# A selective scan block: four of sixteen drive units made on GpSimd as u times B, the opening in halves, the last residual added in HBM

## The reference

```python
x = x + ln(attn(ln(x), ...));  x = x + ln(ffn(ln(x), weight, bias))       # ln: eps 1e-5

def attn(x, ...):                        # d_inner 256, d_state 16, 4 taps
    x_in, z = split(x @ W_in + b_in)
    xc = silu(causal_conv4(x_in) + conv_b)
    Bm, Cm = split(xc @ W_xp + b_xp)     # 16 columns each
    delta = softplus(xc @ W_dt + b_dt)
    dA  = exp(delta[..., None] * -exp(A_log))
    dBx = (delta * xc)[..., None] * Bm[:, :, None, :]
    h_t = dA_t * h_(t-1) + dBx_t;  y_t = sum_s h_t * C_t      # over 256 tokens
    y = (y + D_skip * xc) * silu(z)
    r = x + y @ W_out + b_out
    return alpha * (r - mean(r)) / (std_unbiased(r) + 1e-6) + beta

def ffn(x, weight, bias):                # fake_quant: per-tensor fp8 e4m3 and back
    return fake_quant(x) @ fake_quant(weight).T + bias
```

## Time and profile before

| | |
|---|---|
| median of 3 runs | 639.04 us |
| the profiled execution | 639.14 us |
| its span | 637.4 us |
| PE busy | 542.6 us, 85% |
| DVE busy | 504.8 us, 79% |
| ACT busy | 441.9 us, 69% |
| POOL busy | 300.7 us, 47% |
| transfers of the POOL queue (additions into `acc`) | 33.56 MB, 26.7% of 16 engines |
| transfers of the SP queue | 5.78 MB, 3.3% |

### The profile page before, as it was taken

The page is one execution under the profiler, slowest core; times in us unless marked ns, Lnnn a source line. Parts: engine busy times, 40 slices in busy tenths (PEclk is TensorE's granted clock), DMA queues, the critical chain, the costliest instruction groups (busy, mean ns, idle before and its releaser), DMA issues. The chain is left out here.

```text
span 637.4 us, 10358 instructions
## 1 busy us (share of the span) xinstructions
PE 542.6 (85%) x2893; PEld 419.1 (66%) x2893; DVE 504.8 (79%) x1001; ACT 441.9 (69%) x885; POOL 300.7 (47%) x333
## 2 busy tenths in 40 slices
...
DMA packets 19184, 39.84 MB, mean 62 GB/s; under 512 B 3648, under 2 KB 9920, under 8 KB 19136
## 3 DMA queue, kind: packets, MB, share of 16 engines
q0 software_dynamic: 9216, 33.56, 26.7%
q1 hardware_dynamic: 9920, 5.78, 3.3%
...
## 5 line engine op out<-in xcount | busy, mean ns | idle before, releaser
L1200 DVE TENSOR_TENSOR_SCAN state<-decay,drive 128x512 f32<-128x512 f32 x256 | 297.2, 1203 | 30.7 <-PE drive L995 24.9
L995 PE MATMUL drive<-diag,uT 128*128 128x256 f32 x1024 | 245.9, 384 | 0.7 <-ACT uT L731 0.7
L745 ACT ACTIVATE decay<-delta,a_neg 128x510 f32<-128x510 f32 x256 | 170.5, 730 | 54.8 <-DVE state L1200 53.9
L995 PEld LDWEIGHTS drive<-diag,uT 128*128 128x128 f32 x1024 | 187.1, 193 | 21.7 <-ACT uT L731 1.0
L1011 PE MATMUL hT<-ident,state 128*128 128x128 f32 x1024 | 143.0, 278 | 24.3 <-DVE acc_d L1223 19.1
L1011 PEld LDWEIGHTS hT<-ident,state 128*128 128x128 f32 x1024 | 119.8, 143 | 56.3 <-issue 26.1
L500 POOL TENSOR_SCALAR_AFFINE_SELECT diag<-Bt 128x512 f32<-128x512 f32 x128 | 92.1, 725 | 74.5 <-PE drive L995 58.2
L766 ACT ACTIVATE term<-hT,Ct 128x256 f32<-128x256 f32 x256 | 102.9, 484 | 8.8 <-PE hT L1011 8.8
L516 POOL DMA_DIRECT2D acc<-term x64 | 59.9, 935 | 24.1 <-DMA acc<-term 11.8
L1223 DVE SCALAR_TENSOR_TENSOR acc_d<-hT,Ct,acc_d 128x256 f32<-128x256 f32 x160 | 66.5, 470 | 4.4 <-PE hT L1011 4.3
L938 PE MATMUL fbank<-xnT,w_tap 128*128 128x512 f32 x112 | 50.4, 592 | 0.0
...
## 6 DMA issues: line engine op xcount, KB each, us to landing
acc<-term POOLq DMA_DIRECT2D x64, 512.0 KB, 4.5
out_dram<-state SPq DMA_DIRECT2D x8, 256.0 KB, 2.2
x_all<-in_L_attn_x_dram SPq DMA_DIRECT2D x2, 256.0 KB, 4.2
state<-in_L_attn_conv_w_dram SPq DMA_DIRECT2D x1, 512.0 KB, 5.4
w_in<-in_L_attn_W_in_dram SPq DMA_DIRECT2D x1, 256.0 KB, 3.2
w_dt<-in_L_attn_W_dt_dram SPq DMA_DIRECT2D x1, 256.0 KB, 5.1
...
```

The source lines that it names most:

```text
L745: last = nc.scalar.activation(decay[:, g % DECAYS, h, :, s, 1:], delta[:, par, h, :, 1:], ACT.Exp, scale=a_neg[:, h, SG * g + s:SG * g + s ...
L995: last = nc.tensor.matmul(dst[:, :, P * c:P * c + P], uT[:, par, TC * b + c, P * h:P * h + P], diag[:, n % DIAGS, c, :, :], start=True, st ...
L1200: nc.vector.tensor_tensor_scan(state[:, n % STATES, h, :, :].rearrange("p s t -> p (s t)"), decay[:, g % DECAYS, h, b, :, :].rearrange("p ...
```

## The change

Groups MADE = (2, 5), that is units 4, 5, 10 and 11 of each pair, no longer get a diagonal or a matmul. SP writes the B columns of such a group to HBM in rows (`b_rows`, 1,024 pieces of 4 bytes), loads them back spread over all partitions (`b_all`, 512 KB) and POOL multiplies: `made` = u * B, one operation of 128 x 512 a half. DVE scans these units from `made` in SBUF instead of `drive` in PSUM. `b_all` has one buffer, `made` one for each sequence. The other twelve units keep their way, with LEAD 2 instead of 3 and DIAGS 3 instead of 4. To make room, `pre` shares the memory of `dt_v`, and `ysumT` is gone: the sums stay in `acc`. Twenty-three places in the dictionaries move.

In the opening, `w_tap` is built ahead of the fp8 scaling, the load of `cw_r` goes from seventh to fourth place, Silu reads the bank directly, and the softplus chain, `delta`, `u` (now on DVE) and `uT` run in halves.

In the tail POOL no longer adds the residual: SP stores x1 (the sum behind the first block) to the output during the slots, and POOL issues an additive transfer of each normalized group to HBM, from four buffers.

The diff, cut to its core:

```diff
-LEAD = 3
+LEAD = 2
-DECAYS, DIAGS, STATES, TERMS = 2, 4, 4, 4
+DECAYS, DIAGS, STATES, TERMS = 2, 3, 4, 4
+MADE = (2, 5)
+DRIVEN_G = tuple(g for g in range(DS // SG) if g not in MADE)
-POOL_STEPS = dict(front_root=(3,), front_residual=(24,), front_u=(25,), back_gate=(11,), back_affine=(21,),
-                  back_sum=(25,), sum_states=(6,), back_root=(13, 22, 27))
+POOL_STEPS = dict(front_root=(5,), front_residual=(26,), front_u=(25,), back_gate=(8,), back_affine=(19,),
+                  back_sum=(25,), sum_states=(5,), back_root=(15, 21, 26))
...
             sp.dma_start(w_in[:, :], W_in).then_inc(w_in_loaded, 16)
-            sp.dma_start(bin_c[:, :], column(b_in), **slow).then_inc(w_in_loaded, 16)
+            sp.dma_start(cw_r[:, :, :], conv_w.rearrange("(o d) a k -> o d (a k)", o=1).to_broadcast([P, DI, TAPS])).then_inc(tap_loaded, 16)
...
+            def spread_b(pr, par):
+                sp.wait_ge(bc_ready, nth(pr, 3, 2))
...
+                    sp.dma_start(b_rows[k].rearrange("r p -> p r"),
+                                 Bt[:, par, g, :, :, :].rearrange("p b c s -> p (b c s)"), **slow).then_inc(b_stored[k], 16)
+                for k, g in enumerate(MADE):
+                    sp.wait_ge(b_stored[k], nth(pr, 16, 16))
+                    if k:
+                        sp.wait_ge(made_ready, nth(pr, MADES, PAIR * HALVES * k))
...
+                    sp.dma_start(b_all[:, :, :, :, :].rearrange("p b c s t -> p (b c s t)"),
+                                 b_rows[k].rearrange("(o r) p -> o (r p)", o=1).to_broadcast([P, SG * TOK]))\
+                        .then_inc(b_spread[k], 16)
+            def store_x1(pr):
+                sp.wait_ge(b_sum, nth(pr, 1, 1))
+                sp.dma_start(out_v[:, bass.ds(pr.v * CH, CH), :], x_k[:, bass.ds(pr.v * CH, CH), :]).then_inc(x1_stored, 16)
...
+            def make_drive(pr, par, n):
+                pool.wait_ge(u_ready, nth(pr, 1, 1))
+                pool.wait_ge(b_spread[k], nth(pr, 16, 16))
...
+                for h in range(HALVES):
+                    u_h = u[:, h, L * b:L * b + L].rearrange("p (c t) -> p c t", c=TC).unsqueeze(1).to_broadcast([P, SG, TC, P])
+                    nc.gpsimd.tensor_tensor(made[:, b, h, :, :].rearrange("p s (c t) -> p s c t", c=TC), u_h,
+                                            b_all[:, b, :, :, :].rearrange("p c s t -> p s c t"), ALU.mult).then_inc(made_ready, 1)
             def diag_b(pr, par, n):
+                if g in MADE:
+                    make_drive(pr, par, n)
+                    return
...
-            def last_sum(grp, par):
+            def add_to_out(grp, par):
                 pool.wait_ge(f_norm, nth(grp, 1, 1))
-                nc.gpsimd.tensor_tensor(fo[:, par, :], fn[:, par, :], x_all[:, bass.ds(grp.v * TOK, TOK)], ALU.add)\
-                    .then_inc(f_out, 1)
+                pool.dma_start(out_v[:, CH * grp.v:CH * grp.v + CH, :], chunks(fn[:, grp.v % 4, :]), accum_op=ALU.add)\
+                    .then_inc(stored[grp.v % 4], 16)
...
             for h in range(HALVES):
-                front_xin(Pair(0), h)
+                act.wait_ge(front_full, 1 + h)
+                nc.scalar.activation(xc[:, 0, h, :], front_bank(Pair(0), h), ACT.Silu, bias=in_bias[:, h:h + 1])\
+                    .then_inc(xin_ready, 1)
...
             def drive_unit(pr, par, n):
+                if g in MADE:
+                    return
...
+                if g in MADE:
+                    dve.wait_ge(made_ready, nth(pr, MADES, HALVES * turn(MADE, n) + h + 1))
+                    new = made[:, b, h, :, :].rearrange("p s t -> p (s t)")
+                else:
+                    new = drive[:, m % 2, h, :]
                 nc.vector.tensor_tensor_scan(state[:, n % STATES, h, :, :].rearrange("p s t -> p (s t)"),
                                              decay[:, g % DECAYS, h, b, :, :].rearrange("p s t -> p (s t)"),
-                                             drive[:, n % 2, h, :], 0.0, ALU.mult, ALU.add).then_inc(scan_done, 1)
+                                             new, 0.0, ALU.mult, ALU.add).then_inc(scan_done, 1)
...
+            for h in range(HALVES):
+                dve.wait_ge((half_log, sp_log)[h], 1)
+                nc.vector.tensor_tensor(d[:, h, :], dt_v[:, h, :], dt_e[:, h, :], ALU.max)\
+                    .then_inc((half_delta, delta_ready)[h], 1)
+                dve.wait_ge((half_delta, delta_ready)[h], 1)
+                nc.vector.tensor_tensor(u[:, h, :], d[:, h, :], xc[:, 0, h, :], ALU.mult).then_inc((half_u, u_ready)[h], 1)
```

More of the change, by code:

```diff
@@ L132, in turn, with unit @@
     return PAIR * groups.index(n // PAIR) + n % PAIR
+def unit(groups, j):
+    return PAIR * groups[j // PAIR] + j % PAIR
 def directs(j, s, c):
@@ new lines, in store_x1 @@
+            def store_x1(pr):
+                sp.wait_ge(b_sum, nth(pr, 1, 1))
+                sp.sem_inc(sp_waited, 1)
+                sp.dma_start(out_v[:, bass.ds(pr.v * CH, CH), :], x_k[:, bass.ds(pr.v * CH, CH), :]).then_inc(x1_stored, 16)
+            spread_b(Pair(0), 0)
+            with sp.Fori(0, (PAIRS - 2) // 2) as i:
+                for k in range(2):
+                    pr = Pair(i * 2 + (1 + k), 1 + k)
+                    spread_b(pr, 1 - k)
+                    store_x1(pr.plus(-1))
@@ L454, in _ @@
+            spread_b(Pair(PAIRS - 1), 1)
+            store_x1(Pair(PAIRS - 2))
+            store_x1(Pair(PAIRS - 1))
+            sp.wait_ge(x1_stored, 16 * PAIRS)
+            for k in range(4):
+                sp.wait_ge(stored[k], 16 * PAIRS // 4)
         @block.gpsimd
```

214 lines of the change are left out of this document (131 added, 83 removed).

## The result

The changed kernel takes **670.1 us** (median; 669.6 to 672.1) against 638.0 for the kernel before beside it: ratio **1.049 [1.045, 1.053]**. The forecast was 614.5 with a range to 634: wrong in direction. Its profiled execution has a span of 667.9 us.

The account below looks back on a forecast made before the run. PE was taken to bound slots 0 to 6, DVE slot 7. Opening -8.8, slot 0 -4.6, slots 1 to 6 -7.8, slot 7 +3.5, last back part 0, tail -6.9: -24.6 from 639.1 gives 614.5 us, range 595 to 634.

Parts of the forecast that it names:

- no holding: Rival: scans from SBUF are not held, or wait where DVE idles anyway; 590 us, chance 0.18.
- A slot is 57.4 + 4.2 = 61.6: Slots 1 to 6, before holding: DVE becomes the bound, its 57.4 us of work plus slot 7's idle 4.2.
- PE falls to 54.5: Steady slots: four of sixteen drive units leave PE, 1.91 us each, so PE loses 7.65 us a slot.
- only the edges gain: Rival: middle slots stay at 66.4 us because waits between engines make up the slot; 622 us, chance 0.20.
- The nearest row is 0.44 a time ... I take 3.5: Each slot: eight made scans held by POOL on SBUF cost 3.5 us, bounded by 0 and 10.2.
- POOL takes the bound's place: Rival: each made scan meets a whole POOL read, and POOL's reads wait in turn; 661 us, slower, chance 0.10.
- 3.0 to 6.0, and I take 4.5: Slot 0: time in us for B's store in 4-byte pieces, taken from bin_c's 512 pieces in 3.0.
- Slot 0: First slot: PE relieved, but DVE stalls 3.1 us because B comes late; 57.8 instead of 62.4, -4.6 us.
- Slot 7: Last slot: already bound by DVE, gains nothing and pays for held scans, +3.5 us (0 to +10).
- The opening: Before the first scan: earlier loads and shorter chains, first scan at 34.8 instead of 43.6, -8.8 us.
- The tail: Final groups: POOL's residual addition no longer slows DVE's mask and fshift, -6.9 us; the last addition to HBM counted 0.
- a mean 0.4 above 1.2 us: Sign in slots 1 to 6: made scans average this much while the other scans do not.

Follow-up runs that it names:

- f2: Changed kernel without B's store and load (b_all constant), POOL's products kept, but the scans of the four made units read a drive bank in PSUM: 618.3 us, ratio 0.968.
- e2: Changed kernel with b_all filled once with a constant, so no store, load or wait for B; products and SBUF scans kept: 653.8 us, ratio 1.025.
- f3: Changed kernel without B's store and load and without POOL's products, the four made units' scans reading PSUM: 618.1 us, ratio 0.966.
- e1: Changed kernel with B stored in 128 pieces of 32 bytes a group instead of 1,024 of 4 bytes: 650.9 us, ratio 1.019.
- h1: Changed kernel whole, with its transfers and products, but the four made units' scans read a drive bank in PSUM: 623.7 us, ratio 0.977.
- e3: Changed kernel with no made units: PE drives all sixteen, four diagonal buffers, new places, opening and tail kept: 624.2 us, ratio 0.978.
- f1: Changed kernel without B's store and load and without POOL's products; made is a constant that the four units' scans read in SBUF: 638.9 us, ratio 1.001.

## Why the prediction was wrong, by its steps

A ledger from the forecast to the result, from differences of runs. Without holding and without transfers the forecast was 590 and f2 measured 618.3: 28.3, of which 4.1 a slot, taken six times, are about 25 and the end of the tail some 4. Holding was forecast at 24.5 and is 35.5 (e2 - f2): 11.0. Transfers were forecast at nothing beyond slot 0 and are 16.3 (670.1 - e2). 614.5 + 28.3 + 11.0 + 16.3 = 670.1; it closes because it is a chain of differences. The terms stand for this order of taking things away: with the scans in PSUM the transfers are 5.4 and the holding 46.4.

1. **"A slot is 57.4 + 4.2 = 61.6": failed, about 25 us.** I took slot 7's idle time of DVE as what remains in a middle slot once PE is relieved. f3 and f2 have exactly that state, and a slot is 65.7: in f3 DVE is busy 57.0 us of it, as forecast, and idle 8.7, not 4.2. These four us a slot are waits between the engines; that slot 7 lacks them because no next pair is prepared there is argued, not shown. PE's own relief was smaller as well: "PE falls to 54.5" became 59.1 in f3 and 61.2 in the changed kernel, with granted clocks of 0.95 and 0.93. The rival *only the edges gain* (66.4 a slot, 622) was right on this term. The forecast for f3's state would have been the 590 of the rival *no holding*; it measured 618.
2. **"The nearest row is 0.44 a time ... I take 3.5": the size of a meeting was right, what it does was not; 11 us without transfers.** 64 `made` scans took 64 x (1.601 - 1.203) = 25.5 us extra, 0.40 each (forecast 0.44), and 7 x 3.5 = 24.5 was the forecast for seven slots. But the term priced DVE's side only, and the runs put holding at 35.5 (e2 - f2). POOL's reads are held in turn, twice as much in sum (50 us), and its in-order queue hands that to diagonals, gate and roots; it comes back to DVE as 12.9 us more of waiting. I had that mechanism as the rival *POOL takes the bound's place*, with 661 as its time, and gave it 0.10 because "0.44 is what a meeting costs". `shift` is a 0.16 us instruction: it can be held by POOL, but hardly holds POOL. A scan of 1.2 us does. The row couldn't show the second half.
3. **"3.0 to 6.0, and I take 4.5" for the store, "some 26 us for 10: hidden", and "nothing" for its load on the transfer engines: failed, 16 us.** The two stores took 9.2 us in slot 0 and 11.6 to 12.4 in the later ones, and the addition behind them 12.7 where it had been 5.2 to 5.9; POOL waits for that landing with all its queue. The row I went by, `bin_c`, was one transfer of 512 pieces; here 2,048 pieces go, and in the later slots 512 KB additions with them. The load on the transfer engines was priced in bytes, and should have been in pieces.
4. **Slot 0: half failed.** 61.9 and not 57.8: with the store at 9.2, POOL waited 3.6 us for `b_all` and DVE 5.0 for the root (forecast 3.1), and PE was busy 55.4, not 52.8. **Slot 7: right**, 57.2 against 58.5.
5. **The opening: right.** 35.6 against 34.8; `w_tap` at 8.3 (7.8).
6. **The tail: the gain right, its end wrong.** -6.0 of -6.9, and +4.5 where I wrote 0: I took the landing of an addition as *at most* 4.5 and set it against the whole of addition, store and 2.2; it was 5.1, and 9.0 from the last normalisation to the end.

The forecast's test "a mean 0.4 above 1.2 us" for `made` scans came true in a kernel that lost 5%: a sign that an operation costs what was expected is no sign that the sum holds. The Trainium skill (SBUF — State Buffer, "Who interferes with whom") was read rightly as "all eight scans, and POOL's products too, queue for one port", and the runs agree with that sentence (2.18 and 3.42 us above). My sum left out the second half of it, POOL's products.

A repair that keeps the plan would have to let POOL write its products into the drive banks in PSUM, where f2 scans them for nothing. The Trainium skill (PSUM — Partial Sum Buffer, "The four PSUM rules") says that GpSimd can't touch PSUM at all; no run here shows it, and it wasn't tried.

**Left open.** Why the addition beside the 4-byte stores lands after 12.7 us. It goes with the pieces (the same addition takes 5.8 to 6.4 in e2, 7.8 to 9.1 in e1) and not with held scans: POOL's waits for it are still 48.3 us in h1, where no scan has two SBUF inputs. No run moved the stores to another place of the slot. Twice, where the hardware loop starts its next round, ACT stands too, for 7.84 and 8.6 us, and the profile names nothing for it; these are the two slots of 77 us, the others are 68 to 70. Only a part of that can be this wait: in e3 the same slots are longer too, 68.5 against 64.5.

## What to carry to other kernels

Before work goes from a full engine to one with room, ask where the *consumer* will read the result: moving an operand from PSUM to SBUF turned a scan that nothing in these traces disturbed (1222 ns at most) into one that holds GpSimd and is held by it, and that cost some seven times what the relief of PE brought (46 against 6 us). Price a shared port from both sides, and the slack of a stage by taking the load off without putting it elsewhere (one run, as f3), not from the idle time of a neighbouring stage. Count small transfers by pieces, and look for what waits for the landing of the transfer beside them.

## What the runs showed of the chip

- `tensor_tensor_scan` of 128 x 512 in fp32 takes 1.20 us whether its second input is in PSUM or in SBUF; only with that input in SBUF was it held by a GpSimd operation (up to 3.3 us). The mean was 1.60 beside a POOL busy for 61% of the span, and 1.63 beside one busy for 51% (f1).
- GpSimd paid more than DVE in such meetings, 50 us against 24 (e2 and f2), 43 against 29 (f1 and f3). Means with the scans in PSUM (f2) and in the changed kernel: a diagonal 752 and 979 ns, a root on 4 columns 1029 and 1408 ns, a 1,024-column product 2.36 and 3.22 us.
- 2,048 pieces of 4 B took 9.2 us with no addition in flight and 11.6 to 12.4 with some, and a 512 KB adding transfer beside them 12.7 us where it took 5.2 to 5.9 before. As 512-byte or 32-byte pieces the same bytes cost the kernel nothing (650.9 and 650.9 against 653.8 with no transfer).
- PE's mean granted clock fell from 1.00 to 0.95 (f3) and 0.93 (changed kernel) in the middle slots, when PE idled more (6.6 us of a slot in f3 and 11.7 in the changed kernel, 4.3 before); a 256-column drive matmul went from 382 to 400 and 414 ns.
